# Soft-expert stages: gamma and beta folded into mu and into the copy of the slot sums, norms through TensorE transpositions and column sums, group by group

## The reference, cut to what matters

```python
def _L1_ffn_ref(x, ln_gamma, ln_beta, mu, scale, w1, b1, w2, b2):   # x is _layernorm(x) already
    xn = layernorm(x) * ln_gamma + ln_beta            # over the 128 features
    x_unit = xn / max(norm(xn), 1e-12)                # per token
    mu_unit = mu / max(norm(mu, axis=0), 1e-12)       # 128 x 16 experts x 16 slots
    logits = einsum('bnd,des->bnes', x_unit * scale, mu_unit)
    dispatch = softmax(logits, axis=1)                # over the tokens of a batch
    combine = softmax(logits.reshape(B, N, E * S), axis=-1)
    slot_in = einsum('bnd,bnes->besd', xn, dispatch)
    h = gelu(einsum('besd,edh->besh', slot_in, w1) + b1)
    slot_out = einsum('besh,ehd->besd', h, w2) + b2
    return einsum('besd,bnes->bnd', slot_out, combine)
x = x + 0.5 * _L1_ffn_ref(_layernorm(x), ...)
```

## Time and profile before

| what | value |
|---|---|
| median of 3 runs | 1030.18 us |
| the profiled execution, its time | 1031.45 us |
| its span (first to last instruction) | 1029.7 us |
| TensorE, VectorE, ScalarE, GpSimd busy | 77%, 66%, 50%, 42% of the span |
| mean granted TensorE clock | 0.869 of full speed |

### The profile page before, as it was taken

The page is one execution under the profiler, slowest core; times in us unless marked ns, Lnnn a source line. Parts: engine busy times, 40 slices in busy tenths (PEclk is TensorE's granted clock), DMA queues, the critical chain, the costliest instruction groups (busy, mean ns, idle before and its releaser), DMA issues.

```text
span 1029.7 us, 18855 instructions
## 1 busy us (share of the span) xinstructions
PE 790.1 (77%) x5628; PEld 519.1 (50%) x5628; DVE 680.8 (66%) x2458; ACT 511.1 (50%) x1374; POOL 430.4 (42%) x497
## 2 busy tenths in 40 slices
PE   4689883988499950599748888988988998728977
PEld 3578872647398750377632233333433333316757
DVE  4555555775855539555497677888888887565634
ACT  5323331605043313766311466767767678676660
POOL 1047772400277753311176457566475533261100
PEclk9999997895599985699985588988989899969998
DMA  5831113002011131000032332141232200000002
GB/s 150 238 72 49 49 48 94 1 1 82 15 47 50 49 72 37 0 1 1 1 62 30 52 44 44 29 59 33 34 56 30 44 2 4 2 0 0 2 1 83
DMA packets 53427, 42.97 MB, mean 42 GB/s; under 512 B 9861, under 2 KB 48722, under 8 KB 53328
## 3 DMA queue, kind: packets, MB, share of 16 engines
q1 hardware_dynamic: 46784, 31.74, 15.0%
q0 software_dynamic: 4992, 9.32, 3.3%
q10 hardware_dynamic: 1552, 0.70, 0.3%
HBM read 18.27 MB, written 11.40 MB: 29 GB/s over the span
## 4 chain that ended last, share of the span: by engine, by line
PE 44%; DVE 18%; issue 13%; ACT 10%; POOL 9%; DMA 4%; ACTq 1%; DVEq 0%; SPq 0%; POOLq 0%
PE psum L1448 6%; POOL arena L823 5%; PE psum L1433 4%; PE psum L1388 3%; ACT arena L1606 3%; PE psum L1219 3%; PE psum L740 3%; PE psum L1182 3%; PE psum L1191 2%; DVE cst L1513 2%; PE psum L1420 2%; DMA result_rows<-arena,scatter_row 2%; PE psum L1282 2%; DVE half_stats L441 2%; POOL arena L1064 2%
## 5 line engine op out<-in xcount | busy, mean ns | idle before, releaser
L1513 DVE CUSTOM_DVE_ANT_0 cst<-psum,rot 128x512 bf16<-128x512 f32 (+3 forms) x512 | 222.7, 486 | 54.1 <-PE psum L1420 48.8
L1606 ACT ACTIVATE arena<-psum 128x512 f32<-128x512 f32 (+1 forms) x384 | 177.9, 533 | 61.3 <-PE psum L1433 54.5
L823 POOL DMA_INDIRECT arena<-xhat_rows,gather_row x78 | 77.1, 989 | 154.3 <-DVE scatter_row L640 131.1
L1420 PE MATMUL psum<-arena 48*128 48x512 bf16 (+3 forms) x512 | 123.2, 334 | 17.1 <-DVE row_max L1513 15.9
L1433 PE MATMUL psum<-arena 51*128 51x512 bf16 (+3 forms) x512 | 113.7, 318 | 12.0 <-ACT arena L1606 7.9
L1697 POOL TENSOR_SCALAR_AFFINE_SELECT arena<-arena 128x384 f32<-128x384 f32 x128 | 63.6, 521 | 129.5 <-ACT arena L1606 129.5
L1448 PE MATMUL psum<-arena 128*32 128x512 f32 (+3 forms) x1024 | 100.4, 492 | 1.9 <-POOL arena L1700 1.9
L831 POOL DMA_INDIRECT result_rows<-arena,scatter_row x78 | 78.2, 1002 | 31.6 <-issue 22.0
L790 PE MATMUL psum<-arena 128*128 x624 | 90.8, 289 | 0.1
L778 PE MATMUL psum<-arena 128*128 128x128 f32 x624 | 87.3, 285 | 1.7 <-DVE arena L652 1.6
L711 ACT ACTIVATE arena<-psum,gate_b1T 128x128 f32<-128x128 f32 x156 | 48.9, 364 | 65.3 <-PE psum L778 65.3
(11 more groups left out here) (249 smaller groups left out, 1688.9 us busy)
## 6 DMA issues: line engine op xcount, KB each, us to landing
arena<-cut SPq DMA_DIRECT2D x192, 64.0 KB
xhat_rows<-xh SPq DMA_DIRECT2D x16, 256.0 KB, 2.3
arena<-result_rows SPq DMA_DIRECT2D x8, 512.0 KB, 6.1
x<-in_L_attn_x SPq DMA_DIRECT2D x4, 512.0 KB, 7.4
arena<-in_L_ffn_w SPq DMA_DIRECT2D x1, 2048.0 KB, 9.9
out<-x SPq DMA_DIRECT2D x4, 512.0 KB, 3.2
arena<-xhat_rows,gather_row POOLq DMA_INDIRECT x78, 2.5
result_rows<-arena,scatter_row POOLq DMA_INDIRECT x78, 2.3
```

Of the source, the lines that this page charges most:

```text
L823: pool.indirect_dma_start(xg[:, j % AHEAD, :], None, xhat_dram, bass.IndirectOffsetOnAxis(gather_row[:, j:j + 1], 0)).then_inc(gathered[j ...
L1420: mm = pe.matmul(to[:, col:col + (k + 1) * P], q_stack[b % STACKS][rows, h, k * P:k * P + P], k_stack[b % STACKS][rows, h, 0:(k + 1) * P], ...
L1513: last = nc.vector.tensor_tensor_reduce(masked_scores[:, number % 2, col:col + n_keys], frm[:, col:col + n_keys], mask[:, S - n_keys:], 1. ...
L1606: nc.scalar.activation(prob_e[g % 2][:, j, first:last], bank[MAX_BANKS + number % EXP_BANKS][:, 0:last - first], ACT.Exp, scale=DH ** -0.5 ...
```

## The change

What it does: the normalised tokens are kept as centred value plus 1, so that a row sums to 128. With rest = beta - gamma, gamma times that value plus rest is xn, and a sum over features of rest times mu is the same as rest/128 times the row sum. So mu, once divided by its norm, is multiplied by diag(gamma) + rest/128 (one TensorE product in stage n = 2, `slots_fold_tensor`, copied back by ScalarE, `slots_fold_scalar`), and the slot sums get gamma and rest in `keep_slots`. GpSimd's and VectorE's passes over the tokens are gone. The norm of a token is found otherwise: TensorE transposes the centred tiles of a batch into one bank, ScalarE squares gamma times this plus rest (gamma and rest are per-partition columns there), and TensorE multiplies each squared 128 x 128 block with a column of ones, which gives 128 sums in one column of bank 1. Root, 1/norm and the release of `units` are by group of 8 tiles, four times a stage in place of twice. The fourth group's transpositions and sums come after `logits_d(0)` in TensorE's order. The shift gets one more VectorE instruction per group in the soft-expert stages.

```diff
-        gamma = sb("gamma", [P, D])
-        beta = sb("beta", [P, D])
+        ln_col = sb("ln_col", [P, 4])
+        gamma_col, beta_col, rest_col, mean_col = (ln_col[:, i:i + 1] for i in range(4))
+        fold = carve(arena, 512, (P,))
-        square = carve(arena4, 0, (8, D))
+        square = carve(arena3, 4096, (2, S))
...
+            chain(nc.vector.tensor_tensor(rest_col, beta_col, gamma_col, ALU.subtract))
+            chain(nc.vector.tensor_scalar(mean_col, rest_col, 1.0 / D, None, ALU.mult))
+            nc.vector.tensor_scalar(fold[:], ident, gamma_col, mean_col, ALU.mult, ALU.add)
...
+        def slots_fold_tensor(pe):      # after pe.wait_ge(rows_ready) in stage n == early
+            pe.wait_ge(mix_set[3], 1)
+            pe.matmul(bank[7][:, 0:SLOTS], fold[:], mu[:], start=True, stop=True).then_inc(mix_set[4], 1)
+        def slots_fold_scalar(act):     # before tokens(0, 0) in stage n == early
+            act.wait_ge(mix_set[4], 1)
+            nc.scalar.copy(mu[:], bank[7][:, 0:SLOTS]).then_inc(mix_set[5], 1)
...
+            if stages[n] == "m":        # in stats_finish
+                stats_chain(shift)
+                shift = nc.vector.tensor_scalar(shift_by[:, c], shift_by[:, c], 1.0, None, ALU.add)
...
+            def unit_vector(g):
+                c = slice(GT * g, GT * g + GT)
+                nc.vector.wait_ge(s["norm_sqrt"], at["norm_sqrt"] + g + 1)
+                stats_chain(nc.vector.tensor_scalar(norm[:, c], st[:, 2, c], 1e-12, None, ALU.max))
+                stats_chain(nc.vector.reciprocal(unit[:, c], norm[:, c]))
+                nc.vector.tensor_scalar(unit[:, c], unit[:, c], mscale[:, 0:1], None, ALU.mult).then_inc(s["unit_ready"], 1)
...
+            def squares(act, g):
+                for b in (2 * g, 2 * g + 1):
+                    act.wait_ge(s["front_turned"], at["front_turned"] + b + 1)
+                    if b >= 2:
+                        act.wait_ge(s["norm_mm"], at["norm_mm"] + b - 1)
+                    nc.scalar.activation(square[:, b % 2, :], T_BANK(b)[:], ACT.Square, bias=rest_col, scale=gamma_col).then_inc(s["squared"], 1)
+            def norm_root(act, g):
+                act.wait_ge(s["norm_mm"], at["norm_mm"] + 2 * g + 2)
+                nc.scalar.activation(st[:, 2, GT * g:GT * g + GT], bank[1][:, GT * g:GT * g + GT], ACT.Sqrt).then_inc(s["norm_sqrt"], 1)
+            def turn_front(pe, g):
+                for b in (2 * g, 2 * g + 1):
...                                     # waits for the batch's centred tiles and for squared b - 1
+                    for k in range(TB):
+                        last = pe.transpose(T_BANK(b)[:, k * P:k * P + P], xn[:, TB * b + k, :], ident)
+                    last.then_inc(s["front_turned"], 1)
+            def norms(pe, g):
+                for b in (2 * g, 2 * g + 1):
+                    pe.wait_ge(s["squared"], at["squared"] + b + 1)
+                    for k in range(TB):
+                        last = pe.matmul(bank[1][:, TB * b + k:TB * b + k + 1], square[:, b % 2, k * P:k * P + P], cst[:, C_ONE:C_ONE + 1],
+                                         start=True, stop=True)
+                    last.then_inc(s["norm_mm"], 1)
...
-                    tiles = xn[:, TB * b:TB * b + TB, :]
-                    nc.vector.tensor_tensor(tiles, tiles, beta[:].unsqueeze(1).to_broadcast([P, TB, D]), ALU.add).then_inc(s["xn"], 1)
...
-                    pool.tensor_tensor(tiles, tiles, gamma[:].unsqueeze(1).to_broadcast([P, TB, D]), ALU.mult).then_inc(s["scaled"], 1)
...
-                        nc.scalar.activation(square[:, t % GT, :], xn[:, t, :], ACT.Square, accum_out=st[:, 5, t:t + 1]).then_inc(s["squared"], 1)
...
-                    nc.scalar.copy(slotT[:, :, bass.ds(b, 1), :], bank[1][:, SLOTS:].rearrange("p (e s) -> p e s", e=ME)).then_inc(s["slotT"], 1)
+                    nc.scalar.activation(slotT[:, :, bass.ds(b, 1), :].rearrange("p e o s -> p e (o s)"), bank[1][:, SLOTS:].rearrange("p (e s) -> p e s", e=ME),
+                                         ACT.Identity, bias=rest_col, scale=gamma_col).then_inc(s["slotT"], 1)
...
+                stats_root(act, n, 1)   # ScalarE's order in the front
+                centre(act, 0)
+                stats_root(act, n, 2)
+                squares(act, 0)
+                centre(act, 1)
+                norm_root(act, 0)
+                stats_root(act, n, 3)
+                squares(act, 1)
+                centre(act, 2)
+                norm_root(act, 1)
+                squares(act, 2)
+                centre(act, 3)
+                norm_root(act, 2)
                 copy_xT(0, 0)
-                squares(1)
+                squares(act, 3)
+                norm_root(act, 3)
                 exp_c(0, 0)
...
+                for g in range(GROUPS - 1):   # TensorE's order in the front
+                    turn_front(pe, g)
+                    norms(pe, g)
                 turn_tokens(0, 0)
                 logits_c(0, 0)
                 logits_d(0, 0)
+                turn_front(pe, GROUPS - 1)
+                norms(pe, GROUPS - 1)
                 step(0, 0)
```

More of the change, by code:

```diff
@@ L258, in build @@
         attw_in, att_w = sem("attw_in"), sem("att_w")
-        mixw_in, mix_set = sem("mixw_in"), [sem(f"mix_set{i}") for i in range(4)]
+        mixw_in, mix_set = sem("mixw_in"), [sem(f"mix_set{i}") for i in range(6)]
         x_in = [sem(f"x_in{i}") for i in range(4)]
@@ L571, in vector @@
                 if n == early:
-                    slots_unit_first(dve)
+                    slots_unit_first(dve, chain)
                 dve.wait_ge(s["gated"], at["gated"] + B)
@@ L713, in hidden @@
                     last.then_inc(s["hT_ready_a"], 1)
+                if n == early:
+                    slots_fold_scalar(act)
                 act.wait_ge(s["expert_ready"], at["expert_ready"] + 1)
@@ new lines, in unit_vector @@
+            def unit_vector(g):
+                if ("unit", n, g) in taken:
+                    return
+                taken.add(("unit", n, g))
+                stats_chain.engine = nc.vector
+                norm, unit = st[:, 3, :], st[:, 4, :]
+                c = slice(GT * g, GT * g + GT)
[3 more added lines that the diff above has]
+                nc.vector.tensor_scalar(unit[:, c], unit[:, c], mscale[:, 0:1], None, ALU.mult).then_inc(s["unit_ready"], 1)
@@ new lines, in mix, with once, T_BANK, centre @@
+            between = stages[n - 1] == "f"
+            front_done = set()
+            def once(name, g):
+                if (name, g) in front_done:
+                    return False
+                front_done.add((name, g))
+                return True
+            def T_BANK(b):
+                return bank[(6 if between or b >= 6 else 5) if b % 2 == 0 else 7]
+            def centre(act, g):
+                if not once("centre", g):
+                    return
+                act.wait_ge(ready_sem, GROUPS * n + g + 1)
+                for t in range(GT * g, GT * g + BY_ACT):
+                    nc.scalar.activation(xn[:, t, :], x[:, t, :], ACT.Identity, bias=shift_by[:, t:t + 1],
+                                         scale=rstd[:, t:t + 1]).then_inc(s["centered"], 1)
@@ new lines, in squares @@
+            def squares(act, g):
+                if not once("squares", g):
+                    return
+                for b in (2 * g, 2 * g + 1):
[4 more added lines that the diff above has]
+            def norm_root(act, g):
+                if not once("root", g):
+                    return
+                act.wait_ge(s["norm_mm"], at["norm_mm"] + 2 * g + 2)
+                nc.scalar.activation(st[:, 2, GT * g:GT * g + GT], bank[1][:, GT * g:GT * g + GT], ACT.Sqrt).then_inc(s["norm_sqrt"], 1)
@@ new lines, in turn_front @@
+            def turn_front(pe, g):
+                if not once("turn", g):
+                    return
+                for b in (2 * g, 2 * g + 1):
+                    if b % 2 == 0:
+                        pe.wait_ge(s["centered"], at["centered"] + BY_ACT * g + TB)
+                    else:
+                        pe.wait_ge(s["centered"], at["centered"] + BY_ACT * (g + 1))
+                        pe.wait_ge(s["centered_v"], at["centered_v"] + (GT - BY_ACT) * (g + 1))
+                    if b >= 2:
+                        pe.wait_ge(s["squared"], at["squared"] + b - 1)
+                    for k in range(TB):
+                        last = pe.transpose(T_BANK(b)[:, k * P:k * P + P], xn[:, TB * b + k, :], ident)
+                    last.then_inc(s["front_turned"], 1)
@@ new lines, in norms @@
+            def norms(pe, g):
+                if not once("norms", g):
+                    return
+                for b in (2 * g, 2 * g + 1):
[4 more added lines that the diff above has]
+                    last.then_inc(s["norm_mm"], 1)
@@ L939, in vector, with front_vector @@
+            def front_vector(dve, g):
+                centre_vector(dve, g)
+                if between and g >= 2:
```

(15 more changed lines are left out.)

39 lines of the change are left out of this document (10 added, 29 removed).

## The result

The changed kernel took 1034.05 us (median of 16 runs; one of them, 1101.95 us at a mean granted clock of 0.708 against 0.86 to 0.87 of the others, is left out of the ratio, and the other 15 lie between 1029.74 and 1037.62 with a median of 1034.03), the kernel before 1030.10 us on the same chip (16 runs, 1025.51 to 1032.09). The ratio is 1.0041, 95% interval 1.0028 to 1.0054. That is 3.95 us between the medians; 1034.5 had been predicted. The profiled executions lie further apart, 1037.31 against 1031.45 us, spans 1035.6 and 1029.7, since the one of the changed kernel is 3.3 us above its median; what follows explains this pair, and so 5.9 us.

A forecast was written before the change was run, and what follows sets the result against it. No engine was taken to bound throughout; the chain of waits decides, with TensorE bounding the new front. Terms of 2.75 (first stage), 1.1 (second), 0.38 and 0.1 gave plus 4.35 us: 1034.5 against the median, range 1026 to 1041.

The forecast's parts named there:

- TensorE's level in the front: New front of both soft-expert stages: granted clock 0.50 (1.2 GHz), 5.2 us a group against some 2.6 at full clock.
- A (full clock): TensorE at full clock in the new front, ScalarE the bound: minus 10.6 us, 1019.6; chance 0.12.
- B (cheap narrow products): Front: one-column products cost half of eight-column ones, or the squares' chain is shorter: minus 2.0 us, 1028.2; chance 0.16.
- VectorE's credit: First-stage front: first statistics instruction of groups 2 and 3 falls from 0.66 to 0.17 us, 1.0 us back.
- ScalarE: Prices of its passes: a batch's squaring 0.78 us (bounds 0.59 and 0.9); `keep_slots` plus 0.38 us for two.
- Front of stage 1: First soft-expert stage: logits start 4.1 us earlier, fourth group's pieces follow them; last root plus 0.4 us.
- The second logits: Second `logits_c` runs at the lower clock after a gap: plus 2.35 us in the first stage, plus 0.65 in the second.
- rival C (the clock stays up): Clock stays up through the gap before the second `logits_c`: minus 0.4 us, 1029.8, no change; chance 0.12.
- Front of stage 2: Second soft-expert stage: first tiles at full clock, `logits_c(0)` 4.05 us earlier, last root plus 0.45 us.
- The fold: Before the routed experts' first product: its TensorE product and ScalarE copy cost plus 0.1 us, bounds 0 and 0.6.
- Rival D: Fourth group's sums at the lower clock, 2.1 us more a stage with transpositions: 1038 to 1038.7; within the main case's 0.60.

The follow-up runs named there:

- quarter of the sums: Changed kernel with one four-column product per batch in place of four one-column products, three quarters of the squares left out of the norms; 1024.64 us, ratio 0.995.
- filled gap: Changed kernel plus three unread 128 x 512 fp32 products between `turn_tokens(1)` and `turn_c(0)` of the first step; 1027.01 us, ratio 0.9977.
- filled front: Changed kernel with bf16 squares, fourth group before the first logits, and one unread 512-column product after each of the first three groups' sums; 1014.09 us, ratio 0.9837.

## Why the prediction was right

The direction and the mechanism were as predicted, the total 0.45 us from the median. That it is so close is in part luck: in the profiled pair the terms of the sum came to +6.7 us for a predicted 4.35, since two of them missed by 0.8 and 2.4 us, and what no term had (+1.34, -1.81 and smaller ones) took 0.8 back.

- **TensorE's level in the front.** 0.50, and 3.57 us for 16 narrow instructions (3.42 predicted). Right. Rivals A (full clock) and B (cheap narrow products) are out. The quarter of the sums and the bf16 squares show what B would have been: faster than the kernel before.
- **VectorE's credit.** The 0.66 us of the earlier trace rows went to 0.17 with GpSimd's multiplications gone, as predicted:

```profile
405.15 0.17 DVE L459 TENSOR_TENSOR st<-half_stats 128x8 f32<-128x8 f32 x1
```

- **ScalarE.** A squaring takes 0.773 us on average, 0.78 predicted; `keep_slots` 0.18 and 0.19 us, predicted 0.38 for both.
- **Front of stage 1.** +1.21 from centring to last root for a predicted +0.4. The logits started 4.0 us earlier behind the centring (4.1 predicted), but took 6.6 us (417.73 to 424.36) where 5.8 was taken; the clock rose 5.9 us after their start instead of 4.65, which is 0.6 of the 0.8. The rest is the 3.5 us for the full clock: with the 6.0 us of the kernel before, 3.5 + 3.0 is 6.5, and its logits had taken 6.66. The fourth group's pieces behind them took 3.47 us, 3.57 predicted.
- **The second logits.** Cold in both stages, as forecast: +2.10 for 2.35 and +0.25 for 0.65. The filled gap shows the cause; rival C (the clock stays up) is out.
- **Front of stage 2.** The step that failed, in size: "Its first tiles meet a TensorE that is still at the full clock". They met one at 0.50 (the 8 transpositions at 905.43 took 1.97 us, at the full clock 1.04), so three groups of 5.4 us lay on the chain where two had been counted. +2.66 in place of +0.25 from centring to last root: the logits started 2.3 us earlier behind the centring, not 4.25, and `exp_c(0)` came 2.6 us later behind it than before, not within a microsecond. In five of the seven profiles with the new front (all but this one and the filled front's) these 8 transpositions took 1.42 or 1.43 us, at a granted 1.00. In the profile of the filled gap, whose front is the same code, they and the 16 narrow instructions took 1.7 us less than here, and the logits started 18.13 us behind the centring (898.22), close to the 17.73 of the prediction; here it is 19.68:

```profile
899.92 1.43 PE L1019 MATMUL psum<-cst,arena 128*128 128x128 f32 x8 [0.39 <-ACT arena L988]
...
916.35 3.74 PE L1251 MATMUL psum<-mu,xT 128*128 128x256 f32 x8 [0.67 <-ACT xT L1163]
```

  So the moment of the fall differs from execution to execution, and the term was wrong for this execution more than for the kernel. That may be a part of why the profiled pair lies 5.9 us apart and the medians 3.95; the other executions have no trace.
- **Not foreseen.** The slot network's +1.34 us is the same lottery: in stage 1 that product took between 4.8 us (before) and 6.1. Attention gave back 1.81 us, and 2.6 to 3.2 in the six experiments, so it is no accident of one execution. 0.5 us of it is there when a VectorE instruction ends that took 4.95 us before and now 4.23; both times it ended when GpSimd's fill of memory of 10.48 us did. Where the rest comes from stays open.
- **The fold.** The first product of the experts' stage n = 2 started at 279.24, before at 279.08: 0.16 for 0.1.

```profile
277.33 1.19 PE L426 MATMUL psum<-mu,arena 128*128 128x256 f32 x2 [4.30 <-DVE mu L421]
```

Rival D (sums of the fourth group at the lower level) did not occur: 1.95 us for 16 instructions at 425.67 and at 931.09.

## What to carry to other kernels

Work put on an idle TensorE is not free when it is made of many narrow fp32 products: count instructions (0.21 us each at the lower clock, with 1, 4 or 8 columns), not columns, and ask first whether the operand may be bf16. When a new piece must come before the exponentials, put it ahead of the wide products, not behind them: late pieces delay the exponentials and leave a gap in which the granted clock falls, and the next wide products pay. A stage whose clock is about to change gives a term that no single profile fixes; carry it as a range.

## What the runs showed of the hardware

- Four one-column products in bf16 took 0.26 us from first start to last end; in fp32 eight instructions took some 1.8, at the same granted 0.50. At a granted 1.00 the four in bf16 still took 0.25 us, while 16 in fp32 went from 3.57 to 1.95.
- A TensorE that was busy 3.99 of 4 us with transpositions and one-column products had a granted clock of 0.50; three unread products of 512 columns in a gap kept it at 1.00, and the next `logits_c` at 1.99 in place of 3.78 us.
- With scale and bias taken per partition ScalarE's pass over 128 x 256 from PSUM took 0.57 us where the plain copy took 0.37, and a squaring of 128 x 512 took 0.77 where a plain copy takes 0.59.
